# A two-layer attention and mixture-of-experts kernel: one order of work per engine, found at build time by list scheduling

## The reference

```python
x = L0_attn_x                                   # (4, 512, 128)
xn = _layernorm(x)
x = x + attention0(xn) + moe0(xn)               # 16 heads of 8; RMS norm of q, k; sigmoid gate; output projection
                                                # shared expert + 16 experts of width 64, top 2, softmax weights
xn = _layernorm(x)
x = x + attention1(xn) + moe1(xn)               # 16 heads of 8, no output projection
                                                # 8 experts of width 352, top 2, weights normalized over the two
```

## Time and profile before

| what | us |
|---|---|
| median of 3 executions | 921.08 |
| lowest, highest | 915.45, 922.29 |
| the profiled execution's own time | 915.65 |
| its span, first to last instruction | 913.7 |
| PE busy | 670.5 (73%) |
| DVE busy | 498.9 (55%) |
| ACT busy | 421.5 (46%) |
| POOL busy | 297.7 (33%) |
| mean granted TensorE clock | 0.817 of full |

### The profile page before, as it was taken

One profiled execution on the slowest core, in us unless ns is written; L12 is line 12 of the kernel. 1 busy time (PEld: TensorE's weight loads), 2 busy tenths in 40 slices (PEclk: granted clock), 3 DMA queues, 4 the chain that ended last, 5 costly groups with the idle time before them and its releaser, 6 DMA issues. The chain is left out here.

```text
span 913.7 us, 11538 instructions
## 1 busy us (share of the span) xinstructions
PE 670.5 (73%) x3578; PEld 318.7 (35%) x3578; DVE 498.9 (55%) x1050; ACT 421.5 (46%) x775; POOL 297.7 (33%) x403
## 2 busy tenths in 40 slices
PE   3154876776999998446798777688887878795576
PEld 1122332212344542212223221265555656551122
DVE  4178677744566677446677944443344443366551
ACT  1204545343677776223465433454444444454346
POOL 3305343365122124465300474221212212126430
PEclk9557786676899998667779876798888988899769
DMA  3182011033355422122110142334444344202120
GB/s 102 56 262 92 19 61 62 16 96 93 105 154 163 145 86 77 40 60 77 59 32 31 61 144 90 97 125 141 151 145 148 122 137 149 87 29 76 33 60 13
DMA packets 70827, 84.34 MB, mean 92 GB/s; under 512 B 7184, under 2 KB 58896, under 8 KB 70768
## 3 DMA queue, kind: packets, MB, share of 16 engines
q1 hardware_dynamic: 66672, 75.23, 26.6%
q0 software_dynamic: 4096, 8.40, 3.3%
HBM read 60.13 MB, written 23.46 MB: 91 GB/s over the span
## 5 line engine op out<-in xcount | busy, mean ns | idle before, releaser
L931 DVE TENSOR_REDUCE mx<-slot 128x1 f32<-128x512 f32 x512 | 331.0, 683 | 206.7 <-PE slot L555 156.1
L703 ACT ACTIVATE probsT<-slot 128x512 f32<-128x512 f32 x512 | 284.8, 597 | 223.4 <-PE slot L572 158.1
L572 PE MATMUL slot<-q_stack,k_stack 75*128 75x512 bf16 x512 | 215.2, 426 | 63.8 <-DVE mx L931 52.5
L555 PE MATMUL slot<-k_stack,q_stack 72*128 72x512 bf16 x512 | 218.3, 434 | 32.9 <-DMA k_stack<-parts_hbm 18.6
L584 PE MATMUL pv_ps<-probsT,v 128*32 128x512 f32 x1024 | 160.3, 702 | 2.7 <-issue 0.8
L1018 POOL TENSOR_TENSOR hid<-th,up 128x512 f32<-128x512 f32 (+2 forms) x46 | 58.3, 1268 | 228.3 <-DVE th L797 104.8
L555 PEld LDWEIGHTS slot<-k_stack,q_stack 72*128 72x128 bf16 x512 | 54.3, 106 | 177.7 <-issue 131.7
L533 PE MATMUL slot<-xgT,wbuf 128*128 128x128 f32 (+1 forms) x480 | 75.0, 322 | 36.9 <-DMA wbuf<-in_experts 36.9
L572 PEld LDWEIGHTS slot<-q_stack,k_stack 75*128 75x128 bf16 x512 | 53.7, 106 | 123.2 <-DVE mx L931 63.9
L533 PEld LDWEIGHTS slot<-xgT,wbuf 128*128 128x128 f32 (+1 forms) x480 | 72.0, 226 | 48.5 <-issue 46.1
L797 DVE SCALAR_TENSOR_TENSOR th<-th,slot 128x512 f32<-128x512 f32 (+2 forms) x46 | 31.4, 684 | 101.4 <-ACT th L658 80.5
(11 more groups left out here) (124 smaller groups left out, 598.8 us busy)
## 6 DMA issues: line engine op xcount, KB each, us to landing
wbuf<-in_experts SPq DMA_DIRECT2D x40, 544.0 KB, 5.3
q_stack<-parts_hbm SPq DMA_DIRECT2D x96, 96.0 KB
k_stack<-parts_hbm SPq DMA_DIRECT2D x96, 96.0 KB
parts_hbm<-parts SPq DMA_DIRECT2D x16, 384.0 KB, 2.5
wbuf<-in_experts SPq DMA_DIRECT2D x48, 128.0 KB, 2.1
xg<-xs_hbm SPq DMA_DIRECT2D x22, 256.0 KB, 3.2
ys_hbm<-ys SPq DMA_DIRECT2D x22, 256.0 KB, 2.7
xs_hbm<-zeros SPq DMA_DIRECT2D x1, 3072.0 KB, 15.1
```

The source lines that it names most:

```text
L555: nc.tensor.matmul(ps[:, 0:N], q_stack[0:STACK, h, j * P:(j + 1) * P], k_stack[0:STACK, h, :], start=True, stop=True).then_inc(slot_full, 1)
L572: nc.tensor.matmul(ps[:, 0:N], k_stack[0:STACK + MAXROWS, h, j * P:(j + 1) * P], q_stack[:, h, :], start=True, stop=True).then_inc(slot_fu ...
L703: nc.scalar.activation(probsT[:, k % PROBS, a, :], ps[:, 0:N], ACT.Exp, scale=SCALE).then_inc(slot_free, 1)
L931: nc.vector.tensor_reduce(mx[:, g, u // J, u % J:u % J + 1], ps[:, 0:N], AXIS.X, ALU.max)\
```

## The change

`schedule()` becomes `moments()`: the same hand-written times, but only as the time at which a stage is *wanted*. A new function `tasks()` lists each engine's part of each stage as a task with how long it holds the engine, how long until others can use what it made, and which tasks it needs. `engine_orders()` plays these tasks through event by event: whenever an engine is free, it takes, of the tasks whose needs are met, the one wanted first. What comes out is a list for each engine, and for each PSUM fill the slot that was free at that moment; at most 3 slots hold `M` and at most 3 hold `E`. On the chip each engine still runs its own list strictly in order. "One round per layer" says that all of a layer's tokens are still routed, scattered and gathered at one time.

Three more edits: the row maxima go from `mxT` straight to `q_stack` in three transfers instead of through HBM in two; the weights of a block are wanted 1.5 units before their step, whatever the buffers, and the playing-through holds them back; POOL's `SQ` waits for the `PT` of the sequence before, and the maxima's split on POOL is a stage `MP` of its own.

```diff
-def schedule():
-    at = []
-    def put(time, *found):
-        at.append((time, len(at), found))
+def moments():
+    at = {}
+    def put(time, *stage):
+        at[stage] = time
...
             for u in range(HG * J):
                 put(t - 0.7 + u / 16, "M", A, g, u)
+            put(t + 0.3, "MP", A, g)
             put(t + 0.48, "NT", A, g)
...
-                last_use = t + step * ((b - WBUF[l]) // 4 - q) + down
-                put(max(t - 0.9, last_use + 0.02) if b >= WBUF[l] else t - 1.5, "WL", l, b)
+                put(t - 1.5, "WL", l, b)
...
-    return [found for _, _, found in sorted(at)]
+    return at
+
+AT_ONCE = {"M": 3, "E": 3}
...
+def tasks():
...
+    # add(engine, stage, holds, lasts, *needs, chain=None): a chain keeps its tasks in order
+        add(dve, ("LN", A), 1.75, 1.8, *x_ready, new and (dve, ("XN", A - 1)))
...
+                before = [(pe, ("QK", A - 1, a)) for a in range(2)] + [(dve, ("SS", A - 1))] if new and j == 0 else []
+                add(pe, ("QV", A, j), 0.7, 0.9, (act, ("XT", A)), *before, chain="QV")
...
+            add(pool, ("PT", A, a), 3.6, 3.7, (act, ("HI", A, a)), chain="PT")
...
+            add(sp, ("RF", A, g), 3.4, 5.6, (sp, ("PW", A)), new and (pe, ("PV", A - 1, g, J - 1)), chain="RF")
+            for u in range(HG * J):
+                add(pe, ("M", A, g, u), 0.216, 0.45, u == 0 and (sp, ("RF", A, g)), chain="M")
+                add(dve, ("M", A, g, u), 0.62, 0.75, (pe, ("M", A, g, u)), chain="M")
+            add(pool, ("MP", A, g), 1.7, 1.75, (dve, ("M", A, g, HG * J - 1)), chain="MP")
+            add(pe, ("NT", A, g), 0.25, 0.5, (pool, ("MP", A, g)), chain="NT")
+            add(act, ("NT", A, g), 0.5, 0.65, (pe, ("NT", A, g)), k >= 2 and (sp, ("NT", *k2)), chain="NT")
+            add(sp, ("NT", A, g), 0.75, 3.2, (act, ("NT", A, g)), chain="NT")
...
+                    add(pe, ("E", A, g, j, a), 0.216, 0.45, (sp, ("NT", A, g)), chain="E")
+                    add(act, ("E", A, g, j, a), 0.51, 0.66, (pe, ("E", A, g, j, a)), used, chain="E")
...
+        add(sp, ("ZERO", l), 0.4, 16.0)
...
+            add(pool, ("SC", l, k), 1.96, 4.0, (dve, ("SL", l)), (sp, ("ZERO", l)), chain="SC")
+        for b in range(NB[l]):
+            over = b - WBUF[l]
+            add(sp, ("WL", l, b), 1.15, (3.3, 6.0)[l], (dve, ("SL", l)), over >= 0 and (pe, ("DN", l, over // 4)),
+                l == 1 and b == 0 and (pe, ("DN", 0, Q[0] - 1)), chain="WL")
...
+def engine_orders():
+    found, gated = tasks()
+    waiting = {key: set(task.needs) for key, task in found.items()}
...
+    while True:
+        moved = True
+        while moved:
+            moved = False
+            for engine in ready:
+                if busy[engine] > now:
+                    continue
+                could = ready[engine]
+                if engine == "PE":
+                    could = [key for key in could if key[1][0] not in FILLS or
+                             open_slots and held.get(key[1][0], 0) < AT_ONCE.get(key[1][0], SLOTS)]
+                if not could:
+                    continue
+                key = min(could, key=lambda k: (found[k].wanted, number[k]))
+                ready[engine].remove(key)
+                task = found[key]
+                task.start = now
+                busy[engine] = now + task.holds
+                ends.append((now + task.lasts, key))
+                orders[engine].append(key[1])
+                if engine == "PE" and key[1][0] in FILLS:
+                    ring[key[1]] = open_slots.pop(0)
+                    held[key[1][0]] = held.get(key[1][0], 0) + 1
+                moved = True
...
+    return orders, ring, gated, found
...
-            for stage in plan.order:
+            for stage in plan.orders["SP"]:
...
                     if l == 0:
-                        sp.wait_ge(consts_set, 3)
+                        sp.wait_ge(consts_set, 4)
...
-                    sp.dma_start(hbm["maxima"][A, g], mxT[:, g % 2, :]).then_inc(mx_out, 16)
-                    sp.wait_ge(mx_out, 16 * (A * G + g + 1))
-                    sp.dma_start(q_stack[STACK:STACK + MAXROWS, g * HG:(g + 1) * HG, :],
-                                 hbm["maxima"][A, g].rearrange("(a h) t -> a h t", h=HG)).then_inc(mx_in[g], 16)
+                    for a in range(MAXROWS):
+                        sp.dma_start(q_stack[STACK + a:STACK + a + 1, g * HG:(g + 1) * HG, :],
+                                     mxT[a * HG:(a + 1) * HG, g % 2, :]).then_inc(mx_in[g], 16)
...
-                        pe.wait_ge(mx_in[g], 16 * (A + 1))
+                        pe.wait_ge(mx_in[g], 16 * MAXROWS * (A + 1))
...
+                    if A >= 1:
+                        gp.wait_ge(parts_done, 2 * A)
...
-                elif kind == "M" and stage[3] == HG * J - 1:
+                elif kind == "MP":
```

More of the change, by code:

```diff
@@ L97, in schedule @@
         else:
-            put(t + 0.3, "VG", A, 0)
-            put(t + 0.3, "VG", A, 1)
+            for half in range(2):
+                put(t + 0.3, "VG", A, half)
             for a in range(2):
@@ new lines, with freer @@
+FREED_BY = {"XT": "ACT", "QV": "DVE", "VG": "DVE", "QK": "ACT", "SG": "DVE", "SU": "ACT", "SD": "DVE", "RK": "DVE",
+            "XG": "ACT", "GU": "DVE", "GG": "DVE", "UU": "ACT", "DN": "ACT", "M": "DVE", "NT": "ACT", "E": "ACT",
+            "AT": "DVE", "OT": "ACT", "OY": "DVE"}
+AT_ONCE = {"M": 3, "E": 3}
+def freer(stage):
+    kind = stage[0]
+    if kind in ("SG", "GU", "GG"):
+        return "DVE", ("GA", *stage)
+    if kind == "RK":
+        return "DVE", ("SL", stage[1])
+    return FREED_BY[kind], stage
@@ new lines, in engine_orders @@
+def engine_orders():
+    found, gated = tasks()
+    waiting = {key: set(task.needs) for key, task in found.items()}
+    after = {key: [] for key in found}
+    for key, task in found.items():
+        for need in waiting[key]:
+            after[need].append(key)
+    ready = {engine: [] for engine in ("PE", "ACT", "DVE", "POOL", "SP")}
+    number = {key: k for k, key in enumerate(found)}
+    for key, left in waiting.items():
+        if not left:
+            ready[key[0]].append(key)
+    frees = {freer(stage): stage for engine, stage in found if engine == "PE" and stage[0] in FILLS}
+    busy = {engine: 0.0 for engine in ready}
+    ends = []
+    orders = {engine: [] for engine in ready}
+    ring, open_slots, held = {}, list(range(SLOTS)), {}
+    now = 0.0
+    while True:
[22 more added lines that the diff above has]
+                moved = True
+        if not ends:
+            break
+        later = [time for time in busy.values() if time > now] + [time for time, _ in ends]
+        now = min(time for time in later if time > now) if any(time > now for time in later) else now
+        done = [entry for entry in ends if entry[0] <= now]
+        ends = [entry for entry in ends if entry[0] > now]
+        for _, key in sorted(done):
+            found[key].end = now
+            if key in frees:
+                stage = frees[key]
+                open_slots.append(ring[stage])
+                held[stage[0]] -= 1
+            for other in after[key]:
+                waiting[other].discard(key)
+                if not waiting[other]:
+                    ready[other[0]].append(other)
+    left = [key for key, task in found.items() if task.end is None]
+    assert not left, left[:10]
+    return orders, ring, gated, found
@@ L162, in __init__ @@
-        self.gated = {stage[1:]: k for k, stage in enumerate(x for x in self.order if x[0] == "GA")}
+        for stage in self.orders["PE"]:
+            if stage in self.ring:
+                self.nth[stage] = uses[self.ring[stage]]
+                uses[self.ring[stage]] += 1
     def before(self, a, b):
-        return self.index[a] < self.index[b]
+        return self.orders["DVE"].index(a) < self.orders["DVE"].index(b)
     def down_of(self, n):
-        found = [a for a, k in self.gated.items() if k == n][0]
@@ L170, in down_of @@
-        return {"SG": ("SD", *found[1:]), "GU": ("DN", 0, *found[1:]), "GG": ("DN", 1, *found[1:2])}[found[0]]
+        kind, *rest = self.gated_stages[n]
+        return {"SG": ("SD", *rest), "GU": ("DN", 0, *rest), "GG": ("DN", 1, *rest[:1])}[kind]
 def both_layers(nc, hbm):
@@ L443, in _ @@
             pe.wait_ge(consts_set, 4)
-            for stage in plan.order:
+            for stage in plan.orders["PE"]:
                 kind = stage[0]
@@ L610, in _ @@
             sc.wait_ge(first_in, 64)
-            for stage in plan.order:
+            for stage in plan.orders["ACT"]:
                 kind = stage[0]
@@ L732, in _ @@
             ve.wait_ge(x_in, 16)
-            for stage in plan.order:
+            for stage in plan.orders["DVE"]:
                 kind = stage[0]
@@ L961, in _ @@
             gp.wait_ge(consts_set, 4)
-            for stage in plan.order:
+            for stage in plan.orders["POOL"]:
                 kind = stage[0]
```

171 lines of the change are left out of this document (153 added, 18 removed).

## The result

The changed kernel takes 827.33 us (median of 4; 823.37 to 829.49), the one before 919.94 beside it (median of 4). The ratio is 0.8994, with a 95% interval of 0.8944 to 0.9043: faster by 10%. The forecast was 781, in a range of 715 to 880: direction and range held, the size was too large by half. 93 us came, 135 were forecast.

A forecast was written before the change was run, and what follows sets the result against it. No engine bounds the whole: DVE and PE wait for each other inside one shared order. The seven stretches, 50 + 155 + 100 + 105 + 90 + 207 + 72 = 779, plus 1.95 give 781 us, range 715 to 880.

The forecast's parts named there:

- Zeroing: Zero writes issued first on SP instead of at 47.8 us: gain about 20 us before layer 0's experts.
- Maxima: Row maxima of 32 groups in three direct transfers: -2 us a group, worth up to 9 us.
- Stretch 1: 0 to 50 us, loading and preparing the first sequence, a chain: stays at 50 us.
- Stretches 2, 4, 7: Up to layer 0's experts 188 to 155 us; up to layer 1's last layer norms 152 to 105; final gather 103 to 72.
- Content unchanged: All stretches: the engines' work stays, only idle time goes, so each is sized with its content unchanged.
- Stretch 3: Layer 0's experts with six groups, 104 us, PE full already: 100 us.
- Stretch 5: Routing and scatter of layer 1, 97 us, a chain with POOL's other work between: 90 us.
- Stretch 6: Ten steps of layer 1's experts, 220 us: attention covers the weights' wait, chain 20.7 us a step, 207 us.
- Rival A: Whole kernel: clock stays low, planned durations are off, in-order lists still wait; half the savings, 848 us; chance 0.16.
- Rival B: Engine orders hardly change, only zeroing and maxima gain, 20 + 9: 887 us; chance 0.09.
- Rival C: `E` placed too early on PE, which waits for the maxima; at 5 us a group 941 us; chance 0.08.
- Rival D: PE's clock rises to 1 before layer 0's experts and after them, DVE's 126 and 94 bound: 715 us; chance 0.06.

The follow-up runs named there:

- a_zero_late: Changed kernel with both zero writes planned late again, after the second read of stacked queries and keys: 0.9027 of the kernel before.
- b_zero: Kernel before with only both zero writes issued first on SP: 0.996 of the kernel before.
- a_hbm: Changed kernel with the row maxima going through HBM again in two transfers, SP waiting for the write: 0.8884 of the kernel before.
- a_same: Changed kernel run again unaltered, as yardstick on the chip of other follow-up kernels: 0.8896 of the kernel before.
- a_wl: Changed kernel whose plan lets a weight block's load follow the issue of the block before, not its landing: 0.8798 of the kernel before.
- a_fix_hold: a_fix_all with six weight buffers and three of probabilities again, eased chains and measured durations kept: 0.8647 of the kernel before.
- a_fix: Changed kernel whose plan lets all transfer chains on SP and POOL follow by issue, not landing: 0.867 of the kernel before.
- a_fix_all: Changed kernel with eased transfer chains, eight weight buffers, two of probabilities, and durations as measured on the chip: 721.27 us, 0.8051 of the kernel before.

## Why the prediction was right and where it was wrong

- **What bounds it (rows 1 to 3).** Right: idle time from one shared order, and it went where it was said, DVE's before reductions by 75 us and PE's before `E` by 48, at busy times that changed little (PE 670 to 630 at a mean clock of 0.848 instead of 0.817, DVE 499 to 494).
- **Zeroing, 20 us in stretch 2.** Mis-sized: 14 in the new order, about 1 of the stretch in the old (a_zero_late, b_zero). The step took the SP stall as time on the path; in the old order the second sequence's preparation ran as long.
- **Maxima, up to 9 us.** Nothing that shows in either order (0.9967; a_hbm as good as a_same). That other groups cover it, the reason given, fits. The issues cost 0.6 us each on SP (572/597/732 ns at L653), not the 0.4 of the upper bound.
- **Stretch 1, 50.** 56.6: the other sequences' work, which was to fill DVE's idle time, delays the first one's chain; its transposes of queries start at 33.65 and not at 27.12. Late zero writes bring back nothing that shows: 55.0, where kernels with early ones have 54.8 to 57.3.
- **Stretches 2, 4, 7, forecast 332.** Measured 299, which confirms less than it seems. The step was to size "every stretch with its content unchanged", and stretch 4 held 348 PE instructions instead of 522, so its 90 us do not confirm 105: there luck helped. In 7 the gather sets the end as said, 14 us a round.
- **Content unchanged.** This step failed, and the prediction contradicts it: it lets attention leave stretch 7 for 4 and 5, and adds it to no term. Of the 512 reductions, 111, 87, 98, 59, 97 and 60 started in stretches 2 to 7; now 120, 109, 58, 105, 120 and none do. What left 4 and 7 went mostly to 5, 6 and 3. The misses by stretch come to 114 us and cancel to 49; that the sum is nearer than its terms is luck.
- **Stretch 3, 100.** 115.1. The step said "full already". It was full again, 113 of 115 us, but with more attention in it (109 reductions instead of 87). Gaps between weights that the plan alone has let it in: a_wl, which eases only these, takes it out (89.2).
- **Stretch 5, 90.** 119.4: this step failed. It allowed for "POOL's other work" between scatters; the plan put it there on purpose, with a wait at each, 29 us up to the last scatter:

```profile
POOL mx_neg L1279 <- DVE mx L1183: 19.4, 4, 6.1
POOL mx_neg L1279 <- ACT probsT L955: 10.0, 1, 10.0
```

  The stretch also holds 46 reductions more.
- **Stretch 6, 207.** 237.5: the step that failed outright is "the new plan orders PE's work so, with 6.0 us for the load". The task list gives 6.0 to each of two loads in a row, and the steps that it plans beside attention are 25.4 to 30.4 us; that stood in the list before anything ran. The chain of 20.7 us was right for a step by itself: 20.8 to 22.2 in the last four, as attention ends, and 20.7 to 23.0 everywhere with eased chains and measured durations (a_fix_hold). Eased chains alone (a_fix) leave up to 27.8.
- **Rival A,** half of the savings at 848, came nearer in time than the forecast did. Its mechanism, lists that wait because a task takes longer than planned, is not what holds layer 1's experts in the changed kernel: beside attention, steps and plan agree there within 0.2 us. It does show once the chains are eased: steps of a_fix run up to 6.7 us over the plan, and those of a_fix_hold, with measured durations, at most 0.6. Its sign, a low clock before layer 0's experts, did appear too: 0.75 in stretch 2, where above 0.85 was to refute it. What a full clock there would give was not tried.
- **Rival B** is refuted by the kernels with one part each: 0.996 and 0.9967 where the whole change gives 0.89 to 0.90.
- **Rival C.** PE waited 8.0 us in all for the maxima's transfers, 8.8 before. Not seen in the changed kernel; 32.6 us in a_fix.
- **Rival D**'s figure for 2 and 4 was nearly reached by their sum (235.6 against 126 + 94 = 220), without the clock that it asked for and with less work in 4.

One thing the changed kernel's end says by itself: its last attention is over at 691 us and PE has nothing from 764 on. The span is layer 1's routing, ten steps and the gather, one behind the other from 407 us; for such a chain it is the engines' order, not their load, that counts.

What stays open: why stretches 2 and 5 differ between chips by 18 us each with the same lists. The granted clock differs with them, 0.75 against 0.82 in stretch 2 and 0.84 against 0.88 in 5, but no run shows which follows which. Open too is what would be left to gain over the 0.8051 if stretches 2 and 5 ran at full clock, and whether the chains of arithmetic, which still wait for their results (0.82 us for a reduction in a_fix_all, where the chip takes 0.68), have gaps worth easing.

## What to carry to other kernels

In a build-time scheduler for in-order engines keep apart how long a task holds its engine and when its result can be used: a chain of transfers follows by issue, not by landing. Where it does not, the plan fills the false gaps with other work, and the in-order engines keep to it. Read the plan's own times before the first run: here they gave the steps beside attention within 0.2 us. Then compare its gaps with the trace's (two loads issued 9.5 us apart whose buffers were both free) before looking at priorities. A stall removed counts only if nothing else covers it: try each edit by itself in the old and the new order. The zero writes were worth 0.004 in one and 0.013 in the other, and the same weight buffers 0.015 in one list and 0.05 to 0.06 in the mended one. And when the order changes, do not size a stretch by its old content.
